# Attention weights split on ScalarE and GpSimd instead of GpSimd and VectorE, in a two-layer gated cross-attention model

## The chip, the cores and the metric

The kernel runs on one core of one Trainium2 chip. The metric is device microseconds of that core for one launch, as the median of three runs.

## The reference

The model takes 8 sequences of 100 tokens of width 1024 and a context of 8 x 361 rows, and runs two gated layers. Each layer is an attention to the context and then a feed-forward part:

```python
    x = x + jnp.tanh(g_xattn[0]) * _L0_xattn_ref(_layernorm(x, axis=-1), ctx_4096, L0_xattn_Wq, L0_xattn_Wk, L0_xattn_Wv, L0_xattn_Wo)
    x = x + jnp.tanh(g_ffn[0]) * _L0_ffn_ref(_layernorm(x, axis=-1), L0_ffn_W, L0_ffn_b, L0_ffn_Wq, L0_ffn_Wk, L0_ffn_A, L0_ffn_Bm)
    x = x + jnp.tanh(g_xattn[1]) * _L1_xattn_ref(_layernorm(x, axis=-1), ctx_4096, mask_1x1xSxS2_ff0, L1_xattn_Wq, L1_xattn_Wk, L1_xattn_Wv, L1_xattn_Wo, L1_xattn_q_norm_w, L1_xattn_k_norm_w)
    x = x + jnp.tanh(g_ffn[1]) * _L1_ffn_ref(_layernorm(x, axis=-1), L1_ffn_W_res, L1_ffn_W_pre, L1_ffn_W_post, L1_ffn_H_res_base, L1_ffn_H_pre_base, L1_ffn_H_post_base, L1_ffn_gate, L1_ffn_W_branch)
```

The change touches the two attentions alone. What they compute, of the one of layer 1:

```python
        q = (hidden_states @ Wq.T).reshape(bsz, q_len, H, HD).transpose(0, 2, 1, 3)
...
        q = _rmsnorm(q, q_norm_w)
        k = jnp.repeat(k, GROUPS, axis=1)
        v = jnp.repeat(v, GROUPS, axis=1)
...
        scores = jnp.einsum('bhqd,bhkd->bhqk', q, k) * scale
        scores = scores + attention_mask[:, :, :, :kv_len]
        probs = jax.nn.softmax(scores.astype(jnp.float32), axis=-1).astype(q.dtype)
        out = jnp.einsum('bhqk,bhkd->bhqd', probs, v)
...
        return out @ Wo.T
```

Layer 0 has 16 query heads of 96 in 4 groups that share a key head, and its keys and values also hold the 100 tokens of the sequence itself (461 keys). Layer 1 has 32 query heads of 128 in 8 groups, 361 keys, and norms its queries and keys.

## The kernel before

**Stages.** The kernel first projects the keys and values of the context to DRAM (ahead of 840 us of the span, and for layer 1 between the attention stages), and each attention is one call of `attend()` (lines 819 to 1497), a block in which all five engines run queues of their own that are tied by semaphores alone. Nothing sets the order of the work but the order of the lines written for each engine.

**Two-part numbers.** Every fp32 operand of a matrix product is held as a high part (the value rounded to fp32r) and a low part (value less high part), and each product is three: high x high, low x high, high x low. For a weight tile the raw values come by DMA to `w_raw` (128 x 1024, two slots, `RAW`), the high part goes to `w_hi` and the low part to `w_lo` (three slots each, `SPLIT`). The first three tiles have the high part made by ScalarE (L1128 to 1130, `w_first_done`), the others by GpSimd, as a product with one (`weights(j)`, L1057 to 1064, `w_hi_done`); the low part is always made by VectorE (`split(j)`, L1237 to 1243, `w_lo_done`). The next tile but one for a raw slot is loaded once the low part is made: `tile(j)` of SP waits for `w_lo_done` of tile j - 2. A slot of `w_hi` is free once TensorE has ended the product of tile j - 3. `w_flat` gives 1024 columns for a query tile and for an output tile of layer 1, 768 for an output tile of layer 0.

**Units.** A unit is one batch entry and one group of four heads; `NU` is 32 in layer 0 and 64 in layer 1. Four units (`HB`) make a group of steps, for which the queries are made in 3 or 4 tiles (`QT`), and whose attention output is then multiplied with 4 output tiles, one to a unit, four units later. Keys of a unit come to `k_raw` and values to `v_in`, and GpSimd splits both (`split_keys`, `split_values`); the split values have one buffer, so they can't be written before the value product of the unit before has ended (`pv_done`). In layer 1 the squares of a query tile are split by GpSimd too (`squares`) and summed by TensorE for the norm. Before unit 0, `LEAD` query tiles (6 or 8) are made.

In unit u the engines do, each in this order:

- TensorE: turns (transposes) the probabilities of u in two chunks, scores of unit u+2 for the first pair of heads, first half of the output product of unit u-4, in layer 1 the sums of squares, the remaining turns, second half of the output product, scores of the second pair, value product of u (`weigh_values`, which waits for `v_lo_done`), in some units the turned sums, and one query product. In layer 0 the first unit of every group of four has no query product, and from unit 24 on there is none; the output products start with unit 4, and those of the last four units stand behind the loop.
- ScalarE: copies of turns 0 and 1 (high part of the probabilities, `copy_turn`), exponentials of u+2 for the first pair, copies of the remaining turns, normalisation of u+1, exponentials of the second pair, copy of the attention output (`o_hi`, after `pv_done`), then the query copy (`copy_q`; in layer 1 behind the square).
- VectorE: remainders (low parts) of turns 0 and 1, reciprocal, maxima of u+2 for the first pair, the subtraction for an output tile, accumulation of an output half into `tokens`, remainders of the other turns, accumulation of the other half, maxima of the second pair, the subtraction for the query tile, remainder of the attention output (`o_lo`), remainder of the queries.
- GpSimd: high part of the output tile of unit u+1, split of the values of u, split of the keys of u+3, high part of the query tile of u+1, split of the squares.
- SP: loads of the keys of u+3, of the values of u+2 (after the split of the values of u), of the tiles of u+2.

## Time and profile before

| | us |
|---|---|
| median of three runs | 2654.25 (2653.9 to 2656.74) |
| the profiled execution | 2656.77 |
| its span | 2653.9 |
| TensorE busy | 2424.3 (91%) |
| TensorE weight loads | 2223.6 (84%) |
| VectorE busy | 1448.0 (55%) |
| ScalarE busy | 1072.9 (40%) |
| GpSimd busy | 960.0 (36%) |

Busy time is the time in which an engine executes an instruction; shares are of the span. An engine's average says little by itself, since the stages have different limits: the attention of layer 0 runs from 840 to 1297 us of the span, that of layer 1 from 1520 to 2463. The views used below are the busy time by window (with the clock that TensorE was granted, as a share of full speed), the groups of instructions by source line (L1063 is line 1063), and timelines of single steps. In these PE is TensorE, PEld its weight loads, ACT ScalarE, DVE VectorE, POOL GpSimd; a bracket behind a row is the idle time of that engine before it and what ended it.

### The profile page before, as it was taken

Reading aid. Unit: us, or ns where it says so; the run is one execution under the profiler, and the core shown is the slowest. Engines: PE = TensorE matmul, PEld = TensorE weight load, DVE = VectorE, ACT = ScalarE, POOL = GpSimd, SP = SyncE. Lnnn points to the kernel's source line nnn. Section 1 sums busy time; section 2 is a strip of 40 time slices with the busy share of each in tenths; the row PEclk is TensorE's granted clock in tenths of the full one; section 3 lists DMA queues with packets and bytes.
Section 4 is the critical chain, followed back from the end, with each engine's and each line's share of the span. In section 5 each row is a group of like instructions: output and inputs, shape, how many; then the busy total and the mean of one; then the engine's idle time right before and its main releaser. Section 6 shows DMA issues by size and latency. Waiting matters only on the chain. (4 is left out here: it accounts for less than half of the span.)

```text
span 2653.9 us, 34844 instructions
## 1 busy us (share of the span) xinstructions
PE 2424.3 (91%) x13088; PEld 2223.6 (84%) x13088; DVE 1448.0 (55%) x2329; ACT 1072.9 (40%) x2440; POOL 960.0 (36%) x796
## 2 busy tenths in 40 slices
PE   8999999979998899999869689999999999999834
PEld 6888888768998789998669488999999999998723
DVE  6222222232301467776543456777777777777797
ACT  3122212132211566667310246555555555554423
POOL 3000000000001465664121065776776677666120
PEclk9999999989999899999989899999999999999757
DMA  6222222152333122322021032333333333322001
GB/s 205 72 66 64 67 72 68 45 193 80 114 95 89 52 88 89 91 84 70 21 72 40 20 97 88 98 97 108 98 99 105 106 99 98 108 84 81 6 0 50
DMA packets 159368, 217.54 MB, mean 82 GB/s; under 512 B 31510, under 2 KB 124082, under 8 KB 158178
## 3 DMA queue, kind: packets, MB, share of 16 engines
q1 hardware_dynamic: 159202, 215.33, 26.5%
q8 instruction: 104, 1.70, 0.3%
q14 instruction: 62, 0.51, 0.1%
HBM read 176.99 MB, written 38.29 MB: 81 GB/s over the span
## 5 line engine op out<-in xcount | busy, mean ns | idle before, releaser
L1063 POOL TENSOR_TENSOR attend_w_hi<-attend_w_raw,attend_one 128x1024 fp32r<-128x1024 f32 (+1 forms) x178 | 332.9, 1870 | 158.3 <-DMA attend_w_raw<-in_wo 84.2
L1242 DVE TENSOR_TENSOR attend_w_lo<-attend_w_raw,attend_w_hi 128x1024 fp32r<-128x1024 f32 (+1 forms) x184 | 253.8, 1379 | 207.0 <-ACT attend_w_hi L1130 122.9
L1380 PE MATMUL attend_ps_gemm<-normed_hi,attend_w_hi 128*128 128x400 f32 x704 | 246.1, 350 | 34.0 <-DVE attend_w_lo L1242 34.0
L1146 ACT ACTIVATE attend_p<-attend_p,attend_neg_max 100x361 f32<-100x361 f32 x256 | 150.9, 591 | 258.5 <-DVE attend_neg_max L1281 258.5
L1380 PE MATMUL attend_ps_gemm<-attend_o_hi,attend_w_hi 128*128 128x400 f32 x704 | 249.7, 355 | 4.1 <-issue 4.0
L1380 PE MATMUL attend_ps_gemm<-normed_lo,attend_w_hi 128*128 128x400 f32 x704 | 244.4, 347 | 0.0
L1380 PE MATMUL attend_ps_gemm<-normed_hi,attend_w_lo 128*128 128x400 f32 x704 | 243.4, 346 | 0.0
L1380 PE MATMUL attend_ps_gemm<-attend_o_lo,attend_w_hi 128*128 128x400 f32 x704 | 242.7, 345 | 0.0
L1380 PE MATMUL attend_ps_gemm<-attend_o_hi,attend_w_lo 128*128 128x400 f32 x704 | 242.6, 345 | 0.0
L301 DVE TENSOR_TENSOR context_k_square<-context_k_rows 128x512 f32<-128x512 f32 (+1 forms) x46 | 31.9, 692 | 346.4 <-ACT context_k_rows L226 346.3
L1155 ACT ACTIVATE attend_p<-attend_p,attend_exp_inv 100x361 f32<-100x361 f32 (+1 forms) x384 | 207.7, 621 | 0.0
L1297 DVE TENSOR_TENSOR attend_pt_lo<-attend_ps_turn,attend_pt_hi 121x400 fp32r<-121x400 f32 (+1 forms) x320 | 170.4, 566 | 28.6 <-ACT attend_pt_hi L1194 27.3
L1449 PEld LDWEIGHTS attend_ps_turn<-attend_ident,attend_p 100*121 100x121 f32 (+2 forms) x1280 | 162.8, 182 | 24.6 <-DVE attend_pt_lo L1297 14.7
L615 POOL MEMSET context_mean_w<- 128x128 f32 x1 | 0.2, 205 | 493.9 <-POOLq L57 493.9
L1449 PE MATMUL attend_ps_turn<-attend_ident,attend_p 100*121 100x100 f32 (+2 forms) x1280 | 165.6, 268 | 11.6 <-DVE attend_pt_lo L1297 8.3
L1380 PEld LDWEIGHTS attend_ps_gemm<-normed_hi,attend_w_hi 128*128 128x128 f32 x704 | 134.3, 191 | 36.0 <-issue 34.9
L1089 POOL TENSOR_TENSOR attend_v_lo<-attend_v_in,attend_v_hi 121x384 fp32r<-121x384 f32 x96 | 153.1, 1595 | 7.5
L350 PE MATMUL context_ps_rows<-context_wk_hi,context_ctx_hi 128*128 128x512 f32 (+1 forms) x368 | 146.0, 397 | 10.1 <-DVE context_wk_lo L294 10.1
L1194 ACT ACTIVATE attend_pt_hi<-attend_ps_turn 121x400 fp32r<-121x400 f32 (+1 forms) x320 | 146.3, 504 | 7.5 <-PE attend_ps_turn L1449 6.8
L1437 PE MATMUL attend_ps_score<-attend_k_hi,attend_q_hi 128*100 128x362 f32 (+1 forms) x384 | 140.0, 364 | 9.4 <-ACT attend_p L1143 7.9
L350 PE MATMUL context_ps_rows<-context_wk_lo,context_ctx_hi 128*128 128x512 f32 (+1 forms) x368 | 144.1, 392 | 0.0
L1098 POOL TENSOR_TENSOR attend_square_hi<-attend_q_square,attend_one 128x400 fp32r<-128x400 f32 x64 | 56.3, 880 | 242.5 <-ACT attend_q_square L1167 242.5
(270 smaller groups left out, 6334.8 us busy)
## 6 DMA issues: line engine op xcount, KB each, us to landing
attend_w_raw<-in_wq SPq DMA_DIRECT2D x88, 512.0 KB, 4.2
attend_w_raw<-in_wo SPq DMA_DIRECT2D x64, 512.0 KB, 4.2
attend_w_raw<-in_wo SPq DMA_DIRECT2D x32, 384.0 KB, 3.6
context_ctx_raw<-in_ctxT SPq DMA_DIRECT2D x8, 1456.0 KB, 6.9
attend_k_raw<-scratch_k SPq DMA_DIRECT2D x64, 180.5 KB, 3.7
context_ctx_raw<-in_ctxF SPq DMA_DIRECT2D x22, 512.0 KB
scratch_v<-context_v_out SPq DMA_DIRECT2D x44, 256.0 KB, 2.1
scratch_k<-context_kt_out SPq DMA_DIRECT2D x44, 256.0 KB, 5.1
```

The lines of the kernel that those rows point to most:

```text
L350: mm = pe.matmul(ps_rows[:n, m % ROW_BANKS], x[:, t % CTX, c, 0:n], w[:, c, col], start=(c == 0 and x is ctx_hi and w is w_hi), stop=(c == ...
L1063: pool.tensor_tensor(hi, w_flat(w_raw, j % RAW, j), one[:hi.shape[0]].to_broadcast(hi.shape), ALU.mult).then_inc(w_hi_done, 1)
L1089: pool.tensor_tensor(v_lo[:], v_in[:, slot], v_hi[:].bitcast(F32), ALU.subtract).then_inc(v_lo_done, 1)
L1098: pool.tensor_tensor(square_hi[:], q_square[:], one[:HD].to_broadcast([HD, HT]), ALU.mult).then_inc(square_split, 1)
L1146: act.activation(p[:, slot, h], p[:, slot, h], ACT.Exp, bias=neg_max[:, slot, h:h + 1], accum_out=exp_sum[:, slot, h:h + 1]).then_inc(expe ...
L1155: act.activation(p[:, slot, h], p[:, slot, h], ACT.Copy, scale=exp_inv[:, slot, h:h + 1]).then_inc(p_ready, 1)
L1194: act.activation(pt_hi[:ROWS[kc], kc], ps_turn[:ROWS[kc], kc % 2, :HG * S], ACT.Copy).then_inc(turn_hi_done, 1)
L1242: dve.tensor_tensor(w_flat(w_lo, j % SPLIT, j), w_flat(w_raw, j % RAW, j), w_flat(w_hi, j % SPLIT, j).bitcast(F32), ALU.subtract).then_inc ...
L1297: dve.tensor_tensor(pt_lo[:ROWS[kc], kc], ps_turn[:ROWS[kc], kc % 2, :HG * S], pt_hi[:ROWS[kc], kc].bitcast(F32), ALU.subtract).then_inc(t ...
L1380: mm = pe.matmul(out, left[a](c), right[b](c), start=(c == 0 and a == b == 0), stop=(c == chunks - 1 and a == 1))
L1437: mm = pe.matmul(ps_score[:S, h % 2, :NKE], a[:, i % 2, h, at], b[:, u % K_SLOTS], start=(a is q_hi and b is k_hi), stop=(a is q_lo))
L1449: turn = pe.transpose(ps_turn[:ROWS[kc], kc % 2, h * S:(h + 1) * S], p[:, u % P_SLOTS, h, at:at + ROWS[kc]], ident[:S, :S])
```

## The change

The high part of every weight tile is made by ScalarE, as a copy that rounds, and the low part of every weight tile by GpSimd, as a subtraction. VectorE splits no weights any more, and GpSimd's products with one are gone for the weights. The new `round_weights(j)` of ScalarE takes over the waits for the load and for the slot; `weights(j)` of GpSimd waits for `w_hi_done` and stands in GpSimd's queue where it stood, with the first three tiles added ahead of unit 0. In ScalarE's queue the rounding stands at these places: the first three tiles before everything, then one behind each query copy ahead of unit 0; in a unit the output tile of u+1 behind the copies of turns 0 and 1, and the query tile of u+1 behind the exponentials of the second pair, ahead of the wait for the value product and the copy of the attention output; and the last output tiles behind the loop. TensorE's and SP's queues are as they were.

```diff
--- before.py
+++ after.py
@@ -881,7 +881,6 @@
         ps_out = ps("ps_out", [P, BANK])
         ps_sum = ps("ps_sum", [P, BANK])
         w_load = [sem(f"w_load{slot}") for slot in range(RAW)]
-        w_first_done = sem("w_first_done")
         w_hi_done = sem("w_hi_done")
         w_lo_done = sem("w_lo_done")
         k_load = [sem("k_load0"), sem("k_load1")]
@@ -1055,13 +1054,9 @@
             pool.wait_ge(consts, CONSTS)
 
             def weights(j):
-                pool.wait_ge(w_load[j % RAW], (j // RAW + 1) * 16)
-                if j >= SPLIT:
-                    kind, n = tiles[j - SPLIT]
-                    pool.wait_ge(gemm_done, gemm_at[kind, n, 1 if kind == "o" else 0] + 1)
-                hi = w_flat(w_hi, j % SPLIT, j)
-                pool.tensor_tensor(hi, w_flat(w_raw, j % RAW, j), one[:hi.shape[0]].to_broadcast(hi.shape), ALU.mult
-                                   ).then_inc(w_hi_done, 1)
+                pool.wait_ge(w_hi_done, j + 1)
+                pool.tensor_tensor(w_flat(w_lo, j % SPLIT, j), w_flat(w_raw, j % RAW, j),
+                                   w_flat(w_hi, j % SPLIT, j).bitcast(F32), ALU.subtract).then_inc(w_lo_done, 1)
 
             def split_keys(u):
                 if u >= NU:
@@ -1102,8 +1097,7 @@
                                    ).then_inc(square_split, 1)
 
             for j in range(LEAD):
-                if j >= SPLIT:
-                    weights(j)
+                weights(j)
                 if j >= SPLIT - 1:
                     squares(j - SPLIT + 1)
                 if j == LEAD - 3:
@@ -1125,9 +1119,16 @@
         def _(act):
             act.wait_ge(side_load, 16 * (1 + layer))
             act.activation(gate[:], gate_in[:], ACT.Tanh).then_inc(gated, 1)
+
+            def round_weights(j):
+                act.wait_ge(w_load[j % RAW], (j // RAW + 1) * 16)
+                if j >= SPLIT:
+                    kind, n = tiles[j - SPLIT]
+                    act.wait_ge(gemm_done, gemm_at[kind, n, 1 if kind == "o" else 0] + 1)
+                act.activation(w_flat(w_hi, j % SPLIT, j), w_flat(w_raw, j % RAW, j), ACT.Copy).then_inc(w_hi_done, 1)
+
             for j in range(SPLIT):
-                act.wait_ge(w_load[j % RAW], (j // RAW + 1) * 16)
-                act.activation(w_flat(w_hi, j, j), w_flat(w_raw, j % RAW, j), ACT.Copy).then_inc(w_first_done, 1)
+                round_weights(j)
             act.wait_ge(consts, CONSTS)
 
             def exps(u, pair):
@@ -1195,6 +1196,8 @@
 
             for n in range(LEAD):
                 copy_q(n)
+                if n + SPLIT < LEAD:
+                    round_weights(n + SPLIT)
                 if layer == 1 and n == HG:
                     copy_sums(0)
                     roots(0)
@@ -1209,6 +1212,8 @@
                 i, k = u // HB, u % HB
                 copy_turn(u, 0)
                 copy_turn(u, 1)
+                for j in output_tiles(u + 1)[:1]:
+                    round_weights(j)
                 exps(u + 2, 0)
                 copy_turn(u, 2)
                 if NCH == 4:
@@ -1217,6 +1222,8 @@
                 if layer == 1 and k == 1 and u + HB < NU:
                     copy_sums(i + 1)
                 exps(u + 2, 1)
+                for j in output_tiles(u + 1)[1:SPLIT - 1] + query_tiles(u + 1):
+                    round_weights(j)
                 act.wait_ge(pv_done, u + 1)
                 if i >= 2 and k == 0:
                     act.wait_ge(gemm_done, gemm_at["o", (i - 1) * HB - 1, 1] + 1)
@@ -1229,18 +1236,12 @@
                 if layer == 1 and k == 1 and u + HB < NU:
                     roots(i + 1)
                 copy_q(query_of(u))
+            for j in output_tiles(NU)[SPLIT - 1:]:
+                round_weights(j)
 
         @block.vector
         def _(dve):
             dve.wait_ge(gated, 1)
-
-            def split(j):
-                if j < SPLIT:
-                    dve.wait_ge(w_first_done, j + 1)
-                else:
-                    dve.wait_ge(w_hi_done, j - SPLIT + 1)
-                dve.tensor_tensor(w_flat(w_lo, j % SPLIT, j), w_flat(w_raw, j % RAW, j),
-                                  w_flat(w_hi, j % SPLIT, j).bitcast(F32), ALU.subtract).then_inc(w_lo_done, 1)
 
             def remainder_q(n):
                 if n is None:
@@ -1306,11 +1307,8 @@
                 dve.scalar_tensor_tensor(tokens[:, m, at], ps_gemm[:, gemm_at["o", u, half] % 2, :HT], gate[:],
                                          tokens[:, m, at], ALU.mult, ALU.add).then_inc(o_read, 1)
 
-            for j in range(SPLIT):
-                split(j)
-            for j in range(SPLIT, LEAD):
-                remainder_q(j - SPLIT)
-                split(j)
+            for n in range(LEAD - SPLIT):
+                remainder_q(n)
             remainder_q(LEAD - 3)
             if layer == 1:
                 scales(0)
@@ -1327,8 +1325,6 @@
                 remainder_turn(u, 1)
                 invert(u + 1)
                 maxima(u + 2, 0)
-                for j in output_tiles(u + 1)[:1]:
-                    split(j)
                 if u >= HB:
                     accumulate(u - HB, 0)
                 remainder_turn(u, 2)
@@ -1337,8 +1333,6 @@
                 if HB <= u < NU - 1:
                     accumulate(u - HB, 1)
                 maxima(u + 2, 1)
-                for j in output_tiles(u + 1)[1:SPLIT - 1] + query_tiles(u + 1):
-                    split(j)
                 dve.wait_ge(o_hi_done, (u + 1) * O_COPIES)
                 dve.tensor_tensor(o_lo[:HD, i % 2, :, k * S:(k + 1) * S],
                                   ps_out[:HD, :QT * S].rearrange("p (h t) -> p h t", h=QT),
@@ -1353,12 +1347,9 @@
                     scales(i + 1)
                 remainder_q(query_of(u))
             accumulate(NU - 1 - HB, 1)
-            split(place["o", NU - 2])
             for u in range(NU - HB, NU):
                 for half in range(2):
                     accumulate(u, half)
-                if u == NU - HB:
-                    split(place["o", NU - 1])
 
         @block.tensor
         def _(pe):
```

## Rows read from the trace of the kernel before

**Rows 1.** Busy time by window: window, its length, each engine, clock, DMA.

```profile
840.00:1296.60 456.60, 429.62 (x2432) 395.22 (x2432) 296.36 (x520) 276.08 (x693) 243.63 (x188) 0.96 0.28 81
1520.00:2463.00 943.00, 915.48 (x5376) 889.26 (x5376) 675.13 (x1040) 501.69 (x1221) 642.26 (x521) 0.99 0.31 97
1640.00:2350.00 710.00, 710.00 (x4232) 694.84 (x4231) 530.65 (x819) 391.66 (x956) 503.17 (x403) 1.00 0.33 102
```

**Rows 2.** Groups by line: busy us, mean ns, idle before, releasers.

```profile
L1063 POOL TENSOR_TENSOR attend_w_hi<-attend_w_raw,attend_one 128x1024 fp32r<-128x1024 f32 (+1 forms) x178 | 332.9, 1870 | 158.3 <-DMA attend_w_raw<-in_wo 84.2 <-PE attend_ps_gemm L1380 71.9 <-DMA attend_w_raw<-in_wq 2.3
L1242 DVE TENSOR_TENSOR attend_w_lo<-attend_w_raw,attend_w_hi 128x1024 fp32r<-128x1024 f32 (+1 forms) x184 | 253.8, 1379 | 207.0 <-ACT attend_w_hi L1130 122.9 <-POOL attend_w_hi L1063 84.0
L1130 ACT ACTIVATE attend_w_hi<-attend_w_raw 128x1024 fp32r<-128x1024 f32 x6 | 6.3, 1057 | 11.7 <-DMA attend_w_raw<-in_wq 11.7
L1086 POOL TENSOR_TENSOR attend_v_hi<-attend_v_in,attend_one 121x384 fp32r<-121x384 f32 x96 | 79.5, 828 | 47.5 <-PE attend_ps_out L1461 47.5
```

**Rows 3.** Timeline, GpSimd and VectorE: start, duration, line, operation, count.

```profile
1096.21 1.18 POOL L1076 TENSOR_TENSOR attend_k_lo<-attend_k_raw,attend_k_hi 96x462 fp32r<-96x462 f32 x1
...
1575.82 1.00 POOL L1089 TENSOR_TENSOR attend_v_lo<-attend_v_in,attend_v_hi 121x384 fp32r<-121x384 f32 x1
...
1968.39 1.05 POOL L1101 TENSOR_TENSOR attend_square_lo<-attend_q_square,attend_square_hi 128x400 fp32r<-128x400 f32 x1
1985.29 1.83 DVE L1242 TENSOR_TENSOR attend_w_lo<-attend_w_raw,attend_w_hi 128x1024 fp32r<-128x1024 f32 x1
1986.12 1.90 POOL L1089 TENSOR_TENSOR attend_v_lo<-attend_v_in,attend_v_hi 121x384 fp32r<-121x384 f32 x1
```

**Rows 4.** Timeline of a step in the middle of layer 1.

```profile
1981.62 0.91 ACT L1194 ACTIVATE attend_pt_hi<-attend_ps_turn 121x400 fp32r<-121x400 f32 x2
1985.35 0.60 ACT L1146 ACTIVATE attend_p<-attend_p,attend_neg_max 100x361 f32<-100x361 f32 x1 [2.82 <-DVE attend_neg_max L1281]
1988.60 0.34 PE L1461 MATMUL attend_ps_out<-attend_pt_hi,attend_v_hi 121*128 121x400 f32 x1
1995.29 0.50 ACT L1167 ACTIVATE attend_q_square<-attend_ps_gemm 128x400 f32<-128x400 f32 x1 [1.37 <-PE attend_ps_gemm L1380]
```

**Rows 5.** Timeline, layer 0, from a short step into unit 17.

```profile
1107.02 0.41 ACT L1223 ACTIVATE attend_o_hi<-attend_ps_out 96x300 fp32r<-96x300 f32 x1
1109.63 1.06 DVE L1297 TENSOR_TENSOR attend_pt_lo<-attend_ps_turn,attend_pt_hi 121x400 fp32r<-121x400 f32 x2
1110.25 1.03 PE L1449 MATMUL attend_ps_turn<-attend_ident,attend_p 100*119 100x100 f32 x8
```

**Rows 6.** Timeline: first product of layer 0, unit 0 of layer 1.

```profile
845.72 1.23 DVE L1242 TENSOR_TENSOR attend_w_lo<-attend_w_raw,attend_w_hi 128x1024 fp32r<-128x1024 f32 x1 [108.98 <-ACT attend_w_hi L1130]
847.09 0.67 PE L1380 MATMUL attend_ps_gemm<-normed_hi,attend_w_hi 128*128 128x400 f32 x1 [10.47 <-DVE attend_w_lo L1242]
...
1589.17 0.66 PE L1449 MATMUL attend_ps_turn<-attend_ident,attend_p 100*119 100x100 f32 x4 [1.25 <-DVE attend_pt_lo L1297]
```

**Rows 7.** Timeline, last units of layer 0 and of layer 1.

```profile
1272.69 0.90 ACT L1194 ACTIVATE attend_pt_hi<-attend_ps_turn 121x400 fp32r<-121x400 f32 x2
1275.50 0.41 PE L1461 MATMUL attend_ps_out<-attend_pt_hi,attend_v_hi 121*96 121x400 f32 x1
...
2429.69 1.90 POOL L1063 TENSOR_TENSOR attend_w_hi<-attend_w_raw,attend_one 128x1024 fp32r<-128x1024 f32 x1 [5.57 <-DMA attend_w_raw<-in_wo]
2434.41 0.42 PE L1461 MATMUL attend_ps_out<-attend_pt_hi,attend_v_hi 121*128 121x400 f32 x1 [1.81 <-issue]
2436.73 0.93 ACT L1194 ACTIVATE attend_pt_hi<-attend_ps_turn 121x400 fp32r<-121x400 f32 x2
2439.53 0.43 PE L1461 MATMUL attend_ps_out<-attend_pt_hi,attend_v_hi 121*128 121x400 f32 x1
```

**Rows 8.** Timeline, and a window (columns as in group 1), around a wait in the first steps of layer 1.

```profile
1619.95 0.42 PE L1461 MATMUL attend_ps_out<-attend_pt_hi,attend_v_hi 121*128 121x400 f32 x1 [2.72 <-issue]
...
1616.00:1628.00 12.00, 9.28 (x46) 8.94 (x45) 7.07 (x9) 5.46 (x15) 7.36 (x6) 0.86 0.36 111
```

## The prediction

> **What bounds the kernel now.** The change touches only the two attention stages, so I read first the busy time of each engine over them [rows 1]: 456.6 us for layer 0, 943.0 for layer 1. TensorE is busy for 429.6 and 915.5 us of these, and in the 710 us from 1640 to 2350 it is busy for all 710.00. VectorE (531), ScalarE (392) and GpSimd (503) have room there. So in the long middle of layer 1 nothing that VectorE loses can be given back as time, and all that could ever be won in both stages is TensorE's idle time, 27.0 + 27.5 us. The question is then the opposite one: does a new order of waits open gaps in a TensorE that has none? Second I read the groups of instructions for prices [rows 2], third the timelines of single steps for slack: a step in the middle of layer 1 [rows 4], a short step of layer 0 [rows 5], and the first and last steps of both stages [rows 6 to 8].
>
> **Prices.** Of 184 weight tiles, 178 have their high part made by GpSimd in 1.87 us, 6 by ScalarE in 1.056 us, and all have their low part subtracted by VectorE in 1.38 us on average [rows 2]. After the change ScalarE rounds all 184 and GpSimd subtracts all 184. ScalarE: 1.06 us for 1024 columns and, by columns, 0.8 for the 768 of an output tile of layer 0. A GpSimd subtraction of 1024 columns isn't in the trace. It does the same kind of subtraction on 400 columns in 1.05 us and on 462 in 1.18 [rows 3]: 2.1 ns a column, so 1.05 + 624 x 0.0021 = 2.36 us for 1024, and 1.82 for 768. Below it can't be cheaper than the one-input form of that size, 1.87; above I bound it by the longest stretched subtraction that [rows 3] shows, scaled: the 384 columns that took 1.90 instead of 1.00 us, or 1.9 x 2.36 = 4.5. I take 2.36, because the stretch has a cause that the change removes. The stretched subtraction of the values (1.90) ran beside VectorE's 1.83 us subtraction of the weights; the same one alone took 1.00 [rows 3]. With the weights off VectorE, its other operations in these stages read at most one operand from SBUF beside PSUM, and the trace shows the other GpSimd subtractions at 1.05 beside them.
> The Trainium skill, GPSIMD Engine Reference, section 3.1 (Elementwise), gives 4497 ns for a two-input operation of 2048 fp32 columns against 2293 on VectorE, and advises VectorE for elementwise work: half of it, 2.25 us, would make each term below 0.1 us smaller. Its section 1 (Specifications) says that GpSimd's SBUF interfaces are shared with VectorE operations with two SBUF inputs; by that rule, the trace agrees, 1.90 against 1.00 us.
>
> **Middle of layer 1 (57 of 64 steps, 13.97 us each): nothing.** The chain that counts ends in the value product, which waits for the low part of the values on GpSimd. Its new length, from ScalarE's second turn copy, is: rounding 1.06, weight subtraction 2.36, values high 0.83 and low 1.00, 0.15 between: 5.4 us. In the step shown the copy ends at 1982.53 and the value product starts at 1988.60: 6.07 us [rows 4]. 0.67 is left; before, GpSimd's end at 1988.02 left 0.58 [rows 3]. So the later start of the weights is paid by the values' subtraction losing its stretch. On ScalarE the rounding of the output tile lies in 2.82 us of idle time ahead of the exponentials, and that of the query tile in the 1.37 us ahead of the query square, and that gap is longer in the steps without a table load [rows 4]. GpSimd's second weight then ends some 2.4 us later than VectorE's did, and with it start the transfers behind it on SP (next query tile, keys); they are used over 6 us later. VectorE loses two operations a step, which TensorE doesn't feel.
>
> **Layer 0, first steps of a group (5 of them, units 5, 9, 13, 17, 21): 1.05 each.** The step before has no query product, so it is short, and ScalarE is behind TensorE at its end. Now ScalarE copies the attention output at 1107.02, right after the exponentials, then turns, then VectorE's remainder runs 1109.63 to 1110.19, and TensorE takes the next turn at 1110.25, having waited some 0.1 us [rows 5]. Between the exponentials and 1107.02 the change puts the rounding of a query tile, 1.06 us, and nothing in that chain has slack. 5 x 1.05 = 5.3 us. The other rounding (0.8) falls into the idle time ahead of the exponentials in the middle of the step, as in [rows 4]. From unit 24 on no query tile is left.
>
> **Starts: 1.1 each.** The first product waits for the first tile's low part [rows 6]; VectorE's 1.23 us [rows 6] becomes 2.36. Later tiles come every 4.4 us, slower than ScalarE plus GpSimd need. 2.2 us; in layer 1 0.35 comes back, because VectorE reaches the first maxima without a weight subtraction ahead.
>
> **Layer 1, first steps: 1.4.** In unit 0 TensorE waits 1.25 us for a remainder that follows ScalarE's output copy and turn copy [rows 6], and a rounding now stands ahead of these: +1.06. In units 1 to 3 idle time takes the rounding; in unit 3 GpSimd's longer queue adds some 0.3.
>
> **Last steps.** Here the value product comes early, because there is no query product and no score product to fill the step, and the values' split now stands on GpSimd behind a weight that waits for ScalarE. Layer 0: the chain is 0.8 + 1.82 + 0.83 + 1.00 + 0.15 = 4.6 us; the last unit leaves 1.91 (1273.59 to 1275.50) [rows 7], the one before, by the same pair of lines, 3.6. Stalls 2.7 + 1.0 = 3.7 us. Layer 1: the last unit leaves 1.87 (2437.66 to 2439.53) [rows 7] for 5.4: +3.5. In the unit before it, the tile lands at 2429.69 and the value product starts at 2434.41 [rows 7]: 4.72 us for the same 5.4, since ScalarE has been ready for it by then, so +0.7 if the tile lands as before. It lands later: its transfer is issued behind the values' transfer, which waits for the values' split, so the four units ahead pass on 0.4 us each, 1.6. Together 3.5 + 2.3 = 5.8 us.
>
> **Clock.** Around a wait of 2.72 us TensorE's mean granted clock was 0.86 over 12 us, that is part of them at 1.2 instead of 2.4 GHz [rows 8]: 0.14 x 12 = 1.7 us. The stage ends get three waits that are longer (2.9 to 3.6 us): 3 x 1.7 = 5.1 us. Bounds: 0, as after the wait of 1.81 in [rows 7], which the clock survived, and 2 x 5.1.
>
> **Sum.** Layer 0: 1.1 + 5.3 + 3.7 = 10.1. Layer 1: 1.1 - 0.35 + 1.4 + 5.8 = 7.9. Clock 5.1. +23 us on the profiled execution, 2656.77 us (span 2653.9 and 2.9 around it), 2.5 above the median. On the median: 2654.25 + 23 = 2677 us, +0.9%.
>
> **Rivals.** (a) The gaps are filled (0.13): the 5 mid-stage chains and the tails overlap other waits, and the clock holds. What is left is the two starts and a part of the tails, 2 to 5 us: 2658. For it: the middle of layer 1 really is untouched. Against it: each of the chains ends in a row where TensorE already waits.
> (b) GpSimd is too slow in the middle (0.08). The point from which it decides is a subtraction of 2.36 + 0.67 = 3.0 us; beyond it every one of 57 steps waits. At 3.5 us: 57 x 0.5 = 28 more, 2705; at the upper bound of 4.5, 85 more. For it: no row shows that size on GpSimd. Against it: the rows at 400 and 462 columns lie on one line.
> (c) Faster (0.06): VectorE is what the chains at the stage edges wait for (TensorE's waits there are put down to its remainders and maxima), and freeing it of 254 us shortens them. It would have to sit with a weight subtraction directly ahead of a late operation. That is so at the start of layer 1 alone, 0.35 us there; if it were so in some 20 edge steps at 0.5 us and ScalarE's rounding were hidden, it would be -10: 2644. Against it: in [rows 5] the late operation on VectorE follows ScalarE's copy, not a subtraction of weights.
> Smaller forms of the forecast itself, as no clock loss and half the tails, give 2654 + 23 - 5.1 - 4.7 = 2667; they lie inside its range.
>
> **How the numbers follow.** Forecast 0.73, from 2663 (no clock loss, tails at 5 instead of 9.5) to 2692 (clock at its upper bound, and some of the five chains twice). (a) 0.13, (b) 0.08, (c) 0.06. Of this kernel a measurement tells 0.2% from no change, 5.3 us. Faster 0.06; same 0.13; slower 0.81. The range 2662 to 2693 leaves out (b), (c) and the low part of (a).
>
> **What would show it.** In the profile after: GpSimd's weight subtraction near 2.36 us and the values' low part at 1.00; TensorE still 710 of 710 in the middle of layer 1; its wait for the turn in five steps of layer 0 at 1.1 instead of 0.1; value products that wait for GpSimd in the last two units of each layer, some 3 us in the last one; a granted clock below 1 behind them. The prediction is wrong if the middle of layer 1 has gaps (then (b)), or if the last value product starts less than 2 us behind the last turn copy.

## The result, and the profile after

The changed kernel takes 2681.8 us (median of 4 runs, 2674.07 to 2683.03) against 2654.68 for the kernel before: a ratio of 1.0095, 95% interval 1.0075 to 1.0115. It is slower by 0.95%, where 2677 us, or +0.9%, was forecast. (The ratio is estimated from all runs; the two medians alone are 27.1 us, or 1.02%, apart.) Beside the kernel before on another chip, later, the ratio was 1.0100 (1.0086 to 1.0114). One slow run of the kernel before among those of the experiments, of 5407 us, is in no ratio and no spread given below.

The busy time of the profile after, first by window (columns as in [rows 1]): the attention stage of layer 0 from the end of TensorE's work on the context, that of layer 1 from the end of the norm ahead of it, and 710 us in the middle of layer 1.

```profile
836.40:1310.00 473.60, 434.61 (x2432) 399.55 (x2432) 238.92 (x464) 320.03 (x747) 241.60 (x190) 0.95 0.26 78
1516.60:2488.00 971.40, 920.42 (x5376) 894.11 (x5376) 515.47 (x928) 628.19 (x1356) 656.00 (x528) 0.98 0.30 95
1655.00:2365.00 710.00, 710.00 (x4231) 694.85 (x4230) 390.62 (x714) 486.95 (x1058) 514.52 (x402) 1.00 0.32 101
```

The same two stretches of the kernel before:

```profile
836.60:1296.60 460.00, 429.63 (x2433) 395.22 (x2432) 296.36 (x520) 276.57 (x694) 243.63 (x188) 0.96 0.27 81
1504.10:2463.00 958.90, 915.48 (x5377) 889.26 (x5376) 690.81 (x1056) 508.79 (x1230) 642.26 (x521) 0.98 0.31 96
```

Length less TensorE's busy time is its idle time: 30.4 before and 39.0 after in layer 0, 43.4 and 51.0 in layer 1. So TensorE waits 16.2 us longer in all. The same matrix products also take it 5.0 and 4.9 us longer, 9.9 together. These 26.1 us are the whole loss (the span grew by 25.2; the other stages together are 0.9 us shorter). In the middle of layer 1 TensorE is busy for 710.00 of 710.00 us, as before [rows 1].

The groups of instructions that answer to [rows 2], of after (busy us, mean ns, idle time before and what ended it):

```profile
L1058 POOL TENSOR_TENSOR attend_w_lo<-attend_w_raw,attend_w_hi 128x1024 fp32r<-128x1024 f32 (+1 forms) x184 | 422.3, 2296 | 438.0 <-ACT attend_w_hi L1128 431.9
L1084 POOL TENSOR_TENSOR attend_v_lo<-attend_v_in,attend_v_hi 121x384 fp32r<-121x384 f32 x96 | 97.8, 1019 | 7.5
L1128 ACT ACTIVATE attend_w_hi<-attend_w_raw 128x1024 fp32r<-128x1024 f32 (+1 forms) x184 | 188.5, 1025 | 32.5 <-DMA attend_w_raw<-in_wq 18.1
```

The subtraction takes GpSimd 2.30 us on average over both sizes, ScalarE's rounding 1.03, and GpSimd's subtraction of the values is down to 1.02 from a mean of 1.60, and 1.9 where [rows 3] shows it.

TensorE's waits, of after and then of before (what waited and for what: us in all, times, longest). "issue" means that the profile names no releaser:

```profile
PE attend_ps_gemm L1371 <- POOL attend_w_lo L1058: 36.3, 2, 24.7
PE attend_ps_out L1452 <- issue: 16.1, 10, 3.3
PE attend_ps_turn L1440 <- DVE attend_pt_lo L1298: 14.4, 13, 2.2
```

```profile
PE attend_ps_gemm L1380 <- DVE attend_w_lo L1242: 34.0, 2, 23.5
PE attend_ps_turn L1449 <- DVE attend_pt_lo L1297: 8.3, 9, 1.9
PE attend_ps_out L1461 <- issue: 5.8, 4, 2.7
```

These are the three places of the forecast: the first product of a stage (+2.3 us), the turns that wait for VectorE's remainder behind ScalarE's copy (+6.1), and the value products (+10.3; "issue" hides GpSimd here, as the timeline of the last unit shows). Smaller waits of other kinds became shorter by some 2.5 us. The last unit of layer 1 in the profile after:

```profile
2456.52 1.15 ACT L1195 ACTIVATE attend_pt_hi<-attend_ps_turn 121x400 fp32r<-121x400 f32 x2 [0.27 <-PE attend_ps_turn L1440]
2457.56 1.05 ACT L1128 ACTIVATE attend_w_hi<-attend_w_raw 128x1024 fp32r<-128x1024 f32 x1
2458.69 2.36 POOL L1058 TENSOR_TENSOR attend_w_lo<-attend_w_raw,attend_w_hi 128x1024 fp32r<-128x1024 f32 x1 [5.95 <-ACT attend_w_hi L1128]
2461.01 0.82 POOL L1081 TENSOR_TENSOR attend_v_hi<-attend_v_in,attend_one 121x384 fp32r<-121x384 f32 x1
2461.91 0.99 POOL L1084 TENSOR_TENSOR attend_v_lo<-attend_v_in,attend_v_hi 121x384 fp32r<-121x384 f32 x1
2463.00 0.42 PE L1452 MATMUL attend_ps_out<-attend_pt_hi,attend_v_hi 121*128 121x400 f32 x1 [3.27 <-issue]
```

From the end of the turn copies (2457.67) each row starts where the one above it ends, up to the value product at 2463.00: 5.33 us, where the forecast had 5.4.

The short steps of layer 0 look like this in after (TensorE's turn in unit 17, to be held against the last of [rows 5]); ScalarE's rounding is the row between exponentials and output copy:

```profile
1114.65 1.05 ACT L1128 ACTIVATE attend_w_hi<-attend_w_raw 128x1024 fp32r<-128x1024 f32 x1
1115.60 0.40 ACT L1230 ACTIVATE attend_o_hi<-attend_ps_out 96x300 fp32r<-96x300 f32 x1
...
1118.83 1.03 PE L1440 MATMUL attend_ps_turn<-attend_ident,attend_p 100*119 100x100 f32 x8 [1.05 <-DVE attend_pt_lo L1298]
```

### The profile page after: what moved, and what is told of

Read it like the earlier page. It is cut to its first block and busy times, and to the rows that moved or that the text cites. A ratio compares the mean times of both kernels' runs of the same rounds, so it can differ in the third digit from the quotient of the medians.

```text
span 2679.1 us, 34845 instructions
## 1 busy us (share of the span) xinstructions
PE 2425.0 (91%) x13088; PEld 2225.2 (83%) x13088; DVE 1213.8 (45%) x2145; ACT 1234.4 (46%) x2618; POOL 972.6 (36%) x802
## 5 line engine op out<-in xcount | busy, mean ns | idle before, releaser
L1058 POOL TENSOR_TENSOR attend_w_lo<-attend_w_raw,attend_w_hi 128x1024 fp32r<-128x1024 f32 (+1 forms) x184 | 422.3, 2296 | 438.0 <-ACT attend_w_hi L1128 431.9
L1128 ACT ACTIVATE attend_w_hi<-attend_w_raw 128x1024 fp32r<-128x1024 f32 (+1 forms) x184 | 188.5, 1025 | 32.5 <-DMA attend_w_raw<-in_wq 18.1
L1440 PE MATMUL attend_ps_turn<-attend_ident,attend_p 100*121 100x100 f32 (+2 forms) x1280 | 166.7, 269 | 16.6 <-DVE attend_pt_lo L1298 14.4
L1337 DVE TENSOR_TENSOR attend_o_lo<-attend_ps_out,attend_o_hi 128x400 fp32r<-128x400 f32 (+1 forms) x96 | 51.7, 538 | 275.5 <-ACT attend_o_hi L1230 170.8
L350 PE MATMUL context_ps_rows<-context_wk_hi,context_ctx_lo 128*128 128x512 f32 (+1 forms) x368 | 143.9, 391 | 0.0
```

Of the source, the lines that this page charges most:

```text
L350: mm = pe.matmul(ps_rows[:n, m % ROW_BANKS], x[:, t % CTX, c, 0:n], w[:, c, col], start=(c == 0 and x is ctx_hi and w is w_hi), stop=(c == ...
L1058: pool.tensor_tensor(w_flat(w_lo, j % SPLIT, j), w_flat(w_raw, j % RAW, j), w_flat(w_hi, j % SPLIT, j).bitcast(F32), ALU.subtract).then_in ...
L1128: act.activation(w_flat(w_hi, j % SPLIT, j), w_flat(w_raw, j % RAW, j), ACT.Copy).then_inc(w_hi_done, 1)
L1337: dve.tensor_tensor(o_lo[:HD, i % 2, :, k * S:(k + 1) * S], ps_out[:HD, :QT * S].rearrange("p (h t) -> p h t", h=QT), o_hi[:HD, i % 2, :, ...
L1440: turn = pe.transpose(ps_turn[:ROWS[kc], kc % 2, h * S:(h + 1) * S], p[:, u % P_SLOTS, h, at:at + ROWS[kc]], ident[:S, :S])
```

## The experiments

The theory: the change costs what lengthens three chains at the edges of the stages, on top of it the clock, and nothing in the middle. The rivals: that GpSimd's speed is what counts everywhere, and that VectorE's relief is worth something. The runs came in three groups, each on one chip with its own runs of the kernel before; what is compared across groups goes by the ratio to these. Each ratio has an uncertainty of some 3 to 5 us.

**ScalarE's chain in the short steps.** The rounding of the query tile is moved ahead of the exponentials in units that have no query product of their own:

```diff
-                for j in output_tiles(u + 1)[:1]:
+                early = query_tiles(u + 1) if k == 0 and query_of(u) is None else []
+                for j in output_tiles(u + 1)[:1] + early:
                     round_weights(j)
                 exps(u + 2, 0)
...
-                for j in output_tiles(u + 1)[1:SPLIT - 1] + query_tiles(u + 1):
+                for j in output_tiles(u + 1)[1:SPLIT - 1] + ([] if early else query_tiles(u + 1)):
                     round_weights(j)
```

> The changed kernel with one thing moved: in the first unit of a group that has no query product of its own (units 0, 4, 8, 12, 16, 20 of layer 0 and unit 0 of layer 1) ScalarE rounds the query tile right behind the output tile, ahead of the first exponentials, and no longer ahead of the copy of the attention output. Theory (the rounding lengthens ScalarE's chain, exponentials - output copy - turn copy): the five waits of 1.05 us in units 5, 9, 13, 17, 21 go back to 0.1, unit 1 of layer 0 from 1.56 to 1.09, unit 1 of layer 1 from 2.21 to 1.25, together -6.2 us, some 2675, and a few us less still if the clock in the first steps follows the waits. Rival (GpSimd's longer queue is what delays these steps): the waits stay at 1.05, no change from the changed kernel.

Measured: 2675.42 us, ratio 1.0077 (1.0062 to 1.0092), some 5 us less than the changed kernel. TensorE's waits for VectorE's remainder in turns fall from 13 to 8, 14.4 to 7.8 us:

```profile
PE attend_ps_turn L1441 <- DVE attend_pt_lo L1299: 7.8, 8, 1.9
```

The five waits are gone (0.12 us at most), and unit 1 of layer 1 waits 1.25, as expected. Unit 1 of layer 0 waits 1.17, but a second profile of the changed kernel has 1.19 there without the edit, so this wait is no sign of the edit. Layer 0 as a whole is 5.7 us shorter. Layer 1 gains only 0.6: the 0.96 us won in its unit 1 come back as waits for the next remainder and for the sums in the same unit (0.59 + 0.29 become 1.40 + 0.91). So the chain is shown for layer 0; in the first steps of layer 1 something else is late right behind it.

**The last steps.** GpSimd splits the values ahead of the weight tile wherever no query tile follows (the condition also holds in units 7, 11, 15 and 19 of layer 0, where nothing changed in step length):

```diff
             for u in range(NU):
+                last = u >= HB and not query_tiles(u + 1)
+                if last:
+                    split_values(u)
                 for j in output_tiles(u + 1)[:1]:
                     weights(j)
-                split_values(u)
+                if not last:
+                    split_values(u)
```

> The changed kernel with GpSimd's order turned round in the last units (23 to 31 of layer 0, 56 to 63 of layer 1, where no query tile is left): values first, then the weight tile. Theory (the value product of a last unit waits for a split that stands behind a weight tile, which itself waits for ScalarE): its waits of 0.80 and 2.44 us in layer 0 and 1.27, 1.36, 0.63, 0.84, 2.54 and 3.27 in layer 1 shrink below 0.5 each, -11 us with nothing new, and the half-clock stretches of the two stage ends go, worth 2 to 5 us more: 2665 to 2671. Rival (GpSimd hasn't the time for both, whatever the order): the output products wait for their weights instead by as much, 2677 to 2681.

Measured: 2669.62 us, ratio 1.0055 (1.004 to 1.007), some 11 us less than the changed kernel. The waits of value products fall from ten to two, and these two are in the first steps of layer 1:

```profile
PE attend_ps_out L1456 <- issue: 2.9, 2, 2.4
```

In turn an output product in unit 60 waits 1.73 us, some 1.1 more than the 0.63 us that the value product of that unit had waited; the kernel before has this wait too, 1.38 us. The order in GpSimd's queue is the cause of the waits at the ends, and GpSimd does have the time for both.

**The space in the middle.** Work without use (a product of 128 columns) stands ahead of the values in the middle of layer 1, once in units 8 to 31, three times in units 32 to 55:

```diff
                 for j in output_tiles(u + 1)[:1]:
                     weights(j)
+                if layer == 1 and 8 <= u < 56:
+                    for _ in range(1 if u < 32 else 3):
+                        if fills:
+                            pool.wait_ge(filled, len(fills))
+                        pool.tensor_tensor(pad[:], ident[:], one[:].to_broadcast([P, P]), ALU.mult).then_inc(filled, 1)
+                        fills.append(u)
                 split_values(u)
```

> The changed kernel with work without use on GpSimd between the weight tile and the values of layer 1: one product of 128 columns in units 8 to 31, three in units 32 to 55. One such product should take 0.38 us, with its semaphore 0.45. Theory (the chain weight tile - values - value product has 0.79 us to spare in every middle step of the changed kernel): no wait of TensorE in units 8 to 31, and one of 3 x 0.45 - 0.79 = 0.55 us in each of units 32 to 55, 24 x 0.55 = +13 us on the changed kernel, some 2694. Rival (the space that the profile shows is not real, as the value product is held by something else): no wait in either half, 2681; or, if there is no space, waits in both halves, 24 x 0.45 + 24 x 1.35 = +43 us.

Measured: 2699.42 us, ratio 1.0167 (1.0152 to 1.0182), some 19 us more than the changed kernel by the ratios, where 13 were expected. Windows over a part of the first half and a part of the second, and TensorE's value products from both (start, duration):

```profile
1720.00:2030.00 310.00, 310.00 (x1847) 303.23 (x1846) 171.59 (x314) 213.17 (x461) 232.64 (x197) 1.00 0.32 102
2055.00:2395.00 340.00, 329.09 (x1932) 315.45 (x1931) 179.17 (x328) 222.44 (x484) 261.96 (x254) 1.00 0.30 97
```

```profile
1793.02 0.35 PE L1460 MATMUL attend_ps_out<-attend_pt_hi,attend_v_hi 121*128 121x400 f32 x1
...
1807.05 0.34 PE L1460 MATMUL attend_ps_out<-attend_pt_hi,attend_v_hi 121*128 121x400 f32 x1
...
2091.01 0.32 PE L1436 MATMUL attend_ps_score<-attend_k_lo,attend_q_hi 128*100 128x362 f32 x1
2091.17 0.32 PE L1436 MATMUL attend_ps_score<-attend_k_hi,attend_q_lo 128*100 128x362 f32 x1
2091.98 0.42 PE L1460 MATMUL attend_ps_out<-attend_pt_hi,attend_v_hi 121*128 121x400 f32 x1 [0.49 <-issue]
2092.23 0.35 PE L1460 MATMUL attend_ps_out<-attend_pt_hi,attend_v_lo 121*128 121x400 f32 x1
2092.42 0.34 PE L1460 MATMUL attend_ps_out<-attend_pt_lo,attend_v_hi 121*128 121x400 f32 x1
...
2106.66 0.42 PE L1460 MATMUL attend_ps_out<-attend_pt_hi,attend_v_hi 121*128 121x400 f32 x1 [0.47 <-issue]
```

One filler of 0.40 us costs nothing: no wait in 24 steps, and the time between the end of the values' low part and the value product falls from 0.79 to 0.42. Three (1.37 us) make a wait in each of 24 steps. Where TensorE does wait, it starts 0.10 us after GpSimd's end, so of the 0.79 us some 0.69 are free, and 1.37 less 0.69 is the 0.7 by which a step grew, from 14.0 to 14.7 us. So the space is real, it is some 0.7 us wide, and the rival in which GpSimd is too slow was that near. The waits shown are 0.48 us where 0.55 were expected: a wait that the profile gives as 0.48 costs 0.7. The rows have the difference. TensorE's products start 0.16 to 0.18 us apart and overlap; the last one ahead of the wait is shown for 0.32 us, with nothing beside it at its end, and the first one behind it is followed after 0.25 us.

**One half of the change.** ScalarE makes the high parts as in the changed kernel, VectorE the low parts as before, GpSimd none:

```diff
-                for j in output_tiles(u + 1)[:1]:
-                    weights(j)
                 split_values(u)
...
                 maxima(u + 2, 1)
+                for j in output_tiles(u + 1)[1:SPLIT - 1] + query_tiles(u + 1):
+                    split(j)
                 dve.wait_ge(o_hi_done, (u + 1) * O_COPIES)
```

> One half of the change alone: ScalarE makes all the high parts, at the places of the changed kernel, and VectorE makes all the low parts, at the places of the kernel before; GpSimd has no weights at all. Theory (starts and ends of the stages were lost to GpSimd's subtraction, 2.4 against 1.2 us and ahead of the values; the short steps to ScalarE's rounding): the waits of 1.05 us in units 5, 9, 13, 17, 21 stay, the first product waits 1.1 us less than in the changed kernel in each layer, and the value products of the last units wait for nothing: some 6 us of ScalarE's chain over the kernel before, less the 4 us of waits that the kernel before has itself in its last units, 2657, range 2653 to 2663. The low part of the values takes 1.0 us where VectorE subtracts no weights beside it and up to 1.9 where it does. Rival (relief of VectorE is worth something that is hidden by other losses): then giving the weights back to VectorE adds waits for its remainders in the first and last steps, over 2665.

Measured: 2665.68 us, ratio 1.0038 (1.0024 to 1.0053). It is 10 us over the kernel before and some 15 under the changed one. The starts are those of before, and no value product of the last units waits for GpSimd. But 2657 was missed by 9 us, the time lies where the rival had it (over 2665), and this speaks in part for the rival. TensorE waits longer for turns than in the changed kernel, 17.7 us against 14.4:

```profile
PE attend_ps_turn L1445 <- DVE attend_pt_lo L1293: 17.7, 14, 3.3
```

In unit 17 the reason is in the timeline: VectorE's subtraction, which now waits for ScalarE's rounding, stands ahead of the remainder of the attention output, and the turn waits 1.31 us, not 1.05:

```profile
1110.88 1.05 ACT L1118 ACTIVATE attend_w_hi<-attend_w_raw 128x1024 fp32r<-128x1024 f32 x1
...
1111.96 1.45 DVE L1238 TENSOR_TENSOR attend_w_lo<-attend_w_raw,attend_w_hi 128x1024 fp32r<-128x1024 f32 x1 [2.38 <-ACT attend_w_hi L1118]
...
1115.32 0.86 PE L1445 MATMUL attend_ps_turn<-attend_ident,attend_p 100*119 100x100 f32 x6 [1.31 <-DVE attend_pt_lo L1293]
```

So most of the cost of the first half is ScalarE's chain. And VectorE's relief is worth something once the high part comes from ScalarE: 5 x 0.27 us in these steps, 1.1 in unit 1 of layer 1 (3.32 against 2.21).

**The starts.** The first three low parts of each layer go back to VectorE in the changed kernel, and, as the mirror image, go to GpSimd in the kernel before:

```diff
             for j in range(LEAD):
-                weights(j)
+                if j == SPLIT:
+                    pool.wait_ge(w_lo_done, SPLIT)
+                if j >= SPLIT:
+                    weights(j)
...
+            for j in range(SPLIT):
+                dve.wait_ge(w_hi_done, j + 1)
+                dve.tensor_tensor(w_flat(w_lo, j, j), w_flat(w_raw, j % RAW, j),
+                                  w_flat(w_hi, j, j).bitcast(F32), ALU.subtract).then_inc(w_lo_done, 1)
```

> The changed kernel with the low parts of the first three tiles of each layer back on VectorE. Its first products should start 1.1 us earlier in layer 0 and 1.25 in layer 1, since a subtraction of 1024 columns takes 1.23 us there against 2.39. Theory (a start is worth its own lateness and no more): -2.4 us on the changed kernel. Rival (the later start is also what makes TensorE's clock fall once more in the first steps of layer 0, around 934 to 941 us of the changed kernel, which cost some 3 us): that half-clock stretch goes too, -5 to -6 us.

> The kernel before with the low parts of the first three tiles of each layer on GpSimd, and nothing else changed: the mirror image of giving the starts back. Theory (a start costs its own lateness): +1.1 and +1.25, +2.4 us on the kernel before, with the same half-clock stretches as before in the first steps. Rival (the lateness shifts the waits of the first steps such that the clock falls once more there): +5 to +6 us, with half-clock time in the attention stages above the 26.8 and 15.4 us of the kernel before.

> The changed kernel with the first three low parts of each layer on VectorE, as in the run without late starts, once more, now beside the changed kernel itself on one chip. Theory (a start is worth its own lateness): 2.0 to 2.6 us less than the changed kernel beside it (0.96 and 1.05 us were won at the two starts in the first profile). Rival (what is won at the start is lost again in the first steps, where other waits and the clock decide): no difference.

Measured: 2680.86 us (1.0098, 1.0082 to 1.0113) and, in the repeat, 2677.38 (1.0081, 1.0067 to 1.0094) beside 2683.08 (1.0100) for the changed kernel; the mirror image 2661.93 (1.0021, 1.0012 to 1.003). The first products move by 1.0 to 1.2 us in each layer in all three profiles, as said. The times don't settle more: the gain was nothing once and 5 us once, the loss 5.6 (3.2 to 8.0) where 2.4 was expected. The differences in the first steps are in TensorE's clock, and two profiles of one kernel differ there by as much (next experiment): the mirror image has 33.1 us at 1.2 GHz in the first 115 us of layer 0, the kernel before 26.8 in its first profile and 33.3 in its second. What a late start costs beyond its own 1.1 us stays open.

**The same kernels again.** Both kernels as they are, for a second profile:

> The changed kernel as it is, once more, beside the kernel before on one chip, as the reference for the repeated run without late starts, and for a second profile. If the extra half-clock time of its first steps is of its waits, the second profile shows it again: 36 to 42 us at half clock in the attention stage of layer 0 and 24 to 30 in that of layer 1, ratio 1.009 to 1.010. If it was an accident of one execution, the stretches lie elsewhere and half-clock time falls to the 27 and 15 us of the kernel before in about one of two profiles.

> The kernel before as it is, for a second profile. If its first profile was typical, the attention stages show again 26.8 and 15.4 us at half clock, and three waits of 0.67, 0.57 and 1.81 us ahead of value products in the last units of layer 1. If the profile was of a lucky execution in the first steps and an unlucky one in the last, half-clock time in layer 0 is nearer to the 33 to 38 us that two variants with the same code in these steps showed, and the three waits are shorter. Ratio 1.000 either way, within 0.002.

Measured: 2683.08 us and 1.0100 (1.0086 to 1.0114) for the changed kernel; 2656.03 and 0.9996 (0.9986 to 1.0005) for the kernel before. The attention stages in the second profile of before, and in the second of after:

```profile
837.80:1301.10 463.30, 433.11 (x2432) 397.90 (x2432) 296.59 (x520) 276.46 (x694) 242.22 (x188) 0.96 0.27 80
1508.50:2466.60 958.10, 917.35 (x5377) 891.37 (x5376) 689.41 (x1056) 509.53 (x1231) 637.55 (x529) 0.98 0.31 96
```

```profile
838.10:1313.20 475.10, 437.57 (x2433) 402.45 (x2432) 239.34 (x464) 320.23 (x747) 241.62 (x191) 0.95 0.27 78
1520.30:2491.30 971.00, 920.17 (x5377) 893.80 (x5376) 515.82 (x928) 628.76 (x1356) 656.47 (x530) 0.98 0.31 95
```

Added up from the granted clock of the trace, from the first product of each stage on, TensorE ran at 1.2 GHz for 26.8 and 15.4 us of the two stages in the first profile of before, and for 33.3 and 18.7 in the second; in the changed kernel it was 38.7 and 28.0, then 43.7 and 27.7. So what the change adds in layer 0 is about the same in both pairs, 11.9 and 10.4 us. Its place is not: in the first pair 8.5 us of it lie in the first 115 us of the stage and 3.4 at its end, in the second pair 0.2 and 10.2. Where the clock falls in a given execution is in part chance.

The three waits of 0.67, 0.57 and 1.81 us in the last units of layer 1 of before are absent from the second profile. There GpSimd's subtraction of the values takes 1.0 us in these units, against 1.9 to 2.9 in the first, since it doesn't run beside VectorE's subtraction. In the second pair TensorE waits 17.4 us longer (7.3 and 10.1), and its products take 7.3 us longer.

TensorE's queue is the same in both kernels, so its products can be laid side by side, each with the time until the next one less the idle time between. Where neither kernel ran at 1.2 GHz they take 0.4 us longer in all in the first pair and 0.2 us less in the second. The rest, 9.6 and 7.5 us, stands in and next to stretches at 1.2 GHz. So the longer products are the clock's work and nothing else's.

**Everything mended, and two ways to take only what is good.** First the changed kernel with all three edits:

> The changed kernel with all three edits: early rounding of the query tile in units without a query product, values first in the last units, first three low parts on VectorE. If the three causes are apart and add up: -6 for ScalarE's chain, -12 for the last units, -2.4 for the starts, some 20 us less than the changed kernel: 2660, range 2656 to 2664. The waits of TensorE in the attention stages should then be about those of the kernel before (28.5 and 41.9 us idle) less 3. If the extra half-clock time of the first steps stays, the time lies 2 to 5 us over the kernel before; if it goes, level with it. Rival (relief of VectorE pays once the rest is mended): below the kernel before, under 2650.

Measured: 2663.47 us, ratio 1.0025 (1.0014 to 1.0035), 19 us less than the changed kernel. Alone the three edits gave 5, 11 and between 0 and 5 us, so within the uncertainty the causes add up. TensorE's idle time in its profile is level with the first profile of the kernel before and 4 us above the second. It remains 0.25% over the kernel before; against the first profile of that, all of it is in the clock (37.4 and 22.3 us at 1.2 GHz), against the second about half. VectorE's relief doesn't pay for it.

Then the kernel before, first with values first in the last units (the edit of the second experiment), then with ScalarE making the high parts there:

```diff
+        LATE = place["q", NQ - 1] + 1
...
             def weights(j):
+                if j >= LATE:
+                    return
...
+            def round_weights(j):
+                if j < LATE:
+                    return
+                if j == LATE:
+                    act.wait_ge(w_hi_done, LATE - SPLIT)
```

> The kernel before with GpSimd's order turned round in the last units, values first and then the weight tile, as was done to the changed kernel. Theory (the kernel before loses time at its ends to the same order of GpSimd's queue, a little): its waits of 0.67, 0.57 and 1.81 us ahead of value products in units 58, 59 and 62 of layer 1 go, -3 to -4 us: 2651 to 2652. Rival (in the kernel before a tile's high part on GpSimd is short enough and the value products wait for the tile's landing or something else): no change.

> The kernel before with ScalarE making the high part in the last units alone (every output tile behind the last query tile), VectorE the low part as before, GpSimd only the values and keys there. It is meant as the version that takes from the change what it was good for. Theory (the kernel before waits in units 58, 59 and 62 of layer 1, 0.67, 0.57 and 1.81 us, since GpSimd makes a high part ahead of the values and is stretched by VectorE beside it): these three waits go, with what a wait costs beyond its idle time (0.23 each, as in the filler run) -3.7 us: 0.14% under the kernel before on the same chip. Rival (ScalarE's rounding delays the last units' turn copies instead, as it did the short steps): no gain, or up to +3 us.

Measured: 2663.7 us, ratio 1.0026 (1.0017 to 1.0035), and 2658.37 us, ratio 1.0006 (0.9997 to 1.0015). Both expectations of a gain failed. In the first of the two, the waits for GpSimd in units 58, 59 and 62 of layer 1 do go. (They are absent from the second profile of the kernel before too.) But the weight's high part comes later, VectorE's subtraction waits for it, and the remainder of the turn waits behind that in VectorE's queue. This makes new waits of TensorE of 3.36 us in unit 63, 1.47 in unit 58, and 1.41 where 0.24 was in unit 31 of layer 0. Unit 63 of layer 1, VectorE and then TensorE:

```profile
2446.63 2.90 DVE L1246 TENSOR_TENSOR attend_w_lo<-attend_w_raw,attend_w_hi 128x1024 fp32r<-128x1024 f32 x1 [1.85 <-POOL attend_w_hi L1063]
2449.45 0.62 DVE L1310 SCALAR_TENSOR_TENSOR stream_tokens<-attend_ps_gemm,attend_gate,stream_tokens 128x400 f32<-128x400 f32 x1
2449.99 0.56 DVE L1301 TENSOR_TENSOR attend_pt_lo<-attend_ps_turn,attend_pt_hi 119x400 fp32r<-119x400 f32 x1
...
2450.61 0.70 PE L1465 MATMUL attend_ps_out<-attend_pt_hi,attend_v_hi 119*128 119x400 f32 x1 [3.36 <-DVE attend_pt_lo L1301]
```

The same edit is worth 11 us in the changed kernel and costs 6 in the kernel before: it is only free where VectorE doesn't stand behind the weights. The second aims at waits that the kernel before doesn't have in every execution, and gains nothing that can be measured. No version here beats the kernel before.

## Why the prediction was right, point by point

**Middle of layer 1: right.** The subtraction of 1024 columns takes 2.39 us (2.36 forecast), that of 768 1.83 (1.82), the values' low part 1.02 (1.00). The distance left ahead of the value product is 0.79 us in the middle steps (0.74 to 0.82; 0.67 was forecast, 0.60 was there before). The later weight is indeed paid for by the values' subtraction, which is no longer stretched. By the fillers waits would set in from some 0.7 us of added work, worked out from 0.40 us (none) and 1.37 (in every step): a subtraction of about 3.1 us, where the prediction had 3.0.

**Waits: 18.0 us forecast, 16.2 and 17.4 in the two pairs of profiles.** The terms, in us of added waiting of TensorE:

| term | forecast | first pair | second pair |
|---|---|---|---|
| first products | 2.2 | 2.4 | 2.1 |
| first maxima and steps of layer 1 | 1.05 | 1.3 | 2.5 |
| unit 1 of layer 0 | 0 | 0.45 | 0 |
| five short steps of layer 0 | 5.3 | 4.7 | 4.9 |
| last steps of layer 0 | 3.7 | 2.6 | 1.7 |
| last steps of layer 1 | 5.8 | 4.9 | 6.6 |

(Each is the sum of the idle times over 0.1 us ahead of TensorE's instructions in these units, after less before; one row of the fourth kind and one of the last stand above. There are no such waits in any other unit of either kernel.) The last steps of layer 0 were put too high: the two value products wait 3.2 us (0.80 and 2.44; in the second profile only the last does), but the output product behind them already waited and waits less now, 0.74 against 1.09. In the last steps of layer 1 the last value product waits 3.27 and 3.11 us, where 3.5 was forecast; the rest is spread over the five units ahead of it.

**Clock: the forecast size at the place that was named in one profile, more in the other, and a second place that was not named.** At the ends the granted clock was 1.00 in the kernel before. After the change it is 0.89 over 16 us in layer 0 and 0.90 over 35 us in layer 1:

```profile
1284.00:1300.00 16.00, 12.03 (x59) 10.73 (x59) 6.24 (x14) 5.23 (x11) 7.74 (x6) 0.89 0.15 49
2444.00:2479.00 35.00, 29.19 (x152) 28.68 (x151) 10.13 (x18) 11.96 (x22) 15.41 (x9) 0.90 0.25 79
```

0.11 x 16 + 0.10 x 35 = 5.3 us, against 5.1 forecast. Each fall comes right behind one of three waits of value products, of 2.44, 2.54 and 3.27 us (2.9 to 3.6 were forecast). That the sum is so near is in part luck: the second profile of the changed kernel has 17.1 us at 1.2 GHz at the ends, where the first has 10.2, and part of it stands behind waits of 1.6 and 1.9 us that the kernel before has too, in both profiles without a fall. The second place is the first steps. Products take 9.9 us longer in the first pair and 7.3 in the second, all of it by the clock (above). In the first pair what exceeds the ends' share lies in the first 115 us of both stages. There the change adds 14.3 us at 1.2 GHz in the first pair, 8.5 and 5.8, but only 2.3 in the second, 0.2 and 2.1. The Trainium skill, TensorE: Matmul & The Clock Gate, Part 1 (The HAM clock gate), says that how many products run at the slow clock after a start is "run-variable"; the trace agrees, for stretches in the first steps too: the two profiles of the kernel before have 42.2 and 52.0 us at half clock in the two stages.

**The sum.** Forecast 18.0 + 5.1 = 23. Measured: 16.2 + 9.9 - 0.9 (other stages) = 25.2 in span, and 27.1 between the medians; in the second pair of profiles 17.4 + 7.3 + 1.1 = 25.8. The waits were put somewhat too high and the clock too low, by 5 and 2 us in the two pairs, and they partly cancelled. The range held, but its lower end was set too low for its own reasons: no clock loss and tails at 5 instead of 9.5 us give 2667, not 2663.

**The rivals.** (a), the gaps are filled: each named gap is in the profile, but for the value product of unit 30 of layer 0 in the second. (b), GpSimd too slow: it was 0.7 us a step away. (c), VectorE's relief: it exists, 0.27 us in each of five steps and 1.1 in one, but only against a kernel whose high parts come from ScalarE. With all else mended the time stays 0.25% over the kernel before.

## What to carry to other kernels

Where the bounding engine has no gap in the long middle of a loop, a move of work between the others has nothing to win there. What it changes, it changes at the edges, and here it cost: in the first, the short and the last steps, in which a chain has no other work to hide under. Read the slack there, step by step, not the engines' average load; VectorE stood at 55% and its relief bought nothing. Before a step is put earlier or later in one engine's in-order queue, list what stands behind it: the same reordering was worth 11 us in one kernel and cost 6 in the other.

## What the runs showed of the hardware that was not expected

A wait of TensorE costs more than its idle time says where it interrupts products that overlap. In the filler run 24 waits of 0.48 us made the steps 0.7 us longer each, at a granted clock of 1.00. The changed kernel shows nothing of this beside the kernel before, as both have about as many waits over 0.1 us, 44 and 43 in the first pair.

The slowing of GpSimd beside a VectorE subtraction with both inputs in SBUF hits its products with one too, not only its subtractions. With the high parts on ScalarE and the low ones on VectorE, GpSimd's first step on the keys fell beside that subtraction: a mean of 1.59 us, where the kernel before has 1.07 and the changed kernel 0.85:

```profile
L1063 POOL TENSOR_TENSOR attend_k_hi<-attend_k_raw,attend_one 128x362 fp32r<-128x362 f32 (+1 forms) x96 | 152.5, 1589 | 90.8 <-DMA attend_k_raw<-scratch_k 62.3 <-PE attend_ps_score L1433 28.4
```

```profile
L1068 POOL TENSOR_TENSOR attend_k_hi<-attend_k_raw,attend_one 128x362 fp32r<-128x362 f32 (+1 forms) x96 | 81.2, 846 | 11.2 <-PE attend_ps_score L1428 9.9 <-DMA attend_k_raw<-scratch_k 1.1
```

VectorE can pay too: its subtraction takes 1.23 us alone, 1.83 beside GpSimd's [rows 3], and 2.90 beside a row of GpSimd's work in the run above. But not always. Here it takes its usual time, and GpSimd alone pays, in the run with the high parts on ScalarE (a product that takes 0.79 us alone) and in unit 58 of layer 1 of the kernel before (a subtraction that takes 1.0 alone):

```profile
1995.74 1.22 DVE L1238 TENSOR_TENSOR attend_w_lo<-attend_w_raw,attend_w_hi 128x1024 fp32r<-128x1024 f32 x1
1995.78 1.83 POOL L1063 TENSOR_TENSOR attend_k_hi<-attend_k_raw,attend_one 128x362 fp32r<-128x362 f32 x1
...
2391.10 2.85 POOL L1089 TENSOR_TENSOR attend_v_lo<-attend_v_in,attend_v_hi 121x384 fp32r<-121x384 f32 x1
2391.85 1.22 DVE L1242 TENSOR_TENSOR attend_w_lo<-attend_w_raw,attend_w_hi 128x1024 fp32r<-128x1024 f32 x1
```

In unit 58 GpSimd's row had even begun first. What decides who pays stays open.

Executions of one kernel on this chip differ by several us (2647.4 to 2660.4 over 22 runs of the kernel before in one group), and a single profile shows one of them; the two profiles of the kernel before differ in the clock of the first steps and in the waits of the last. Three waits that the first profile of the kernel before had, 3 us in all, were not in the second.
